# Row maxima of the attention: from two transfers per half batch to two ScalarE copies into four operand rows

## What is computed

```python
qkv = x @ w_qkv + b_qkv                       # q, k, v: 8 texts, 16 heads, 256 rows, 16 numbers
att = jnp.einsum('bhqd,bhkd->bhqk', q, k) * scale
att = jnp.where(causal, att, -jnp.inf)
att = jax.nn.softmax(att, axis=-1)            # over the keys
y = jnp.einsum('bhqk,bhkd->bhqd', att, v)
x = _layernorm(x + y @ w_proj + b_proj)
```

## Time and profile before

| what | us |
|---|---|
| three runs | 664.5, 667.37, 670.26 |
| median | 667.37 |
| span of the profiled execution | 664.9 |
| TensorE busy | 621.7 (93%) |
| VectorE busy | 493.7 (74%) |
| ScalarE busy | 327.0 (49%) |
| GpSimd busy | 225.2 (34%) |

### The profile page before, as it was taken

The page is one execution under the profiler, slowest core; times in us unless marked ns, Lnnn a source line. Parts: engine busy times, 40 slices in busy tenths (PEclk is TensorE's granted clock), DMA queues, the critical chain, the costliest instruction groups (busy, mean ns, idle before and its releaser), DMA issues.

```text
span 664.9 us, 13964 instructions
## 1 busy us (share of the span) xinstructions
PE 621.7 (93%) x5064; PEld 565.3 (85%) x5064; DVE 493.7 (74%) x1039; ACT 327.0 (49%) x734; POOL 225.2 (34%) x274
## 2 busy tenths in 40 slices
PE   5988998998999999999999999999999998899996
PEld 4766787776767989999899998999989988799996
DVE  4755474674764788879888799887999888767653
ACT  5444553553575355655556555565566644231320
POOL 9402332432453251422223232232312213352543
PEclk9799898997999999999999999999999999999999
DMA  8634646357400040010000000000000000042240
GB/s 283 203 103 146 173 135 190 93 173 217 121 18 1 1 160 0 2 33 2 0 0 0 32 0 0 0 0 0 0 1 1 1 1 1 16 147 82 80 157 34
DMA packets 31374, 43.34 MB, mean 65 GB/s; under 512 B 3072, under 2 KB 18912, under 8 KB 31328
## 3 DMA queue, kind: packets, MB, share of 16 engines
q1 hardware_dynamic: 31328, 42.73, 21.1%
HBM read 29.39 MB, written 13.21 MB: 64 GB/s over the span
## 4 chain that ended last, share of the span: by engine, by line
PE 56%; DVE 13%; issue 13%; DMA 5%; SPq 5%; POOL 4%; ACT 3%; DVEq 0%; POOLq 0%; ACTq 0%
PE bank L448 26%; PE bank L2171 11%; PE bank L1991 4%; POOL hid_hl L801 3%; DMA k_rows<-k_hl 3%; PE bank L1891 2%; DMA q_op<-negT 2%; PE bank L1977 1%; PE bank L456 1%; PE bank L1849 1%; PE bank L2008 1%; SPq L519 1%; PE bank L1856 1%; PE bank L1872 1%; PE bank L2000 1%
## 5 line engine op out<-in xcount | busy, mean ns | idle before, releaser
L448 PE MATMUL bank<-slots_hl,whhT_hl 128*128 128x256 f32 x864 | 113.1, 284 | 0.0
L448 PEld LDWEIGHTS bank<-slots_hl,whhT_hl 128*128 128x128 f32 x864 | 105.5, 188 | 2.4 <-ACT gate_z L1104 1.0
L1293 DVE TENSOR_REDUCE neg_max<-bank 128x2 f32<-128x512 f32 (+1 forms) x96 | 65.7, 690 | 55.2 <-PE bank L1858 41.3
L2171 PE MATMUL bank<-attn_hl,vg_hl 128*128 128x256 f32 x864 | 105.7, 280 | 0.1
L2171 PEld LDWEIGHTS bank<-attn_hl,vg_hl 128*128 128x128 f32 x864 | 100.9, 188 | 4.3 <-ACT attn_hl L815 3.9
L870 ACT ACTIVATE pT<-bank 128x512 f32<-128x512 f32 x96 | 56.9, 598 | 57.7 <-PE bank L1872 41.7
L682 POOL TENSOR_SCALAR_AFFINE_SELECT pT<-pT 128x512 f32<-128x512 f32 x64 | 40.6, 638 | 117.5 <-ACT pT L870 117.4
L696 POOL TENSOR_TENSOR sq<-sq 128x256 f32<-128x256 f32 x24 | 18.1, 754 | 170.6 <-ACT sq L1089 130.3
L801 POOL TENSOR_TENSOR hid_hl<-hid,hid_hl 128x512 fp32r<-128x512 f32 x32 | 40.9, 1303 | 25.8 <-ACT hid_hl L815 25.7
L448 PE MATMUL bank<-x2T_hl,keys_hl 128*128 128x256 f32 x384 | 48.6, 284 | 0.0
L448 PE MATMUL bank<-values_hl,hid_hl 128*128 128x256 f32 x384 | 47.8, 281 | 0.3 <-DVE x L1567 0.3
(11 more groups left out here) (212 smaller groups left out, 1298.2 us busy)
## 6 DMA issues: line engine op xcount, KB each, us to landing
gate_rows<-gate_mem SPq DMA_DIRECT2D x48, 128.0 KB, 3.1
q_rows<-q_hl SPq DMA_DIRECT2D x21, 256.0 KB
k_rows<-k_hl SPq DMA_DIRECT2D x21, 256.0 KB
q_op<-q_rows SPq DMA_DIRECT2D x28, 192.0 KB, 3.2
k_op<-k_rows SPq DMA_DIRECT2D x14, 384.0 KB, 4.4
x_in<-in_x_dram SPq DMA_DIRECT2D x8, 256.0 KB, 6.6
c_in<-in_ctx_dram SPq DMA_DIRECT2D x8, 256.0 KB, 4.8
out_dram<-y_out SPq DMA_DIRECT2D x8, 256.0 KB, 2.8
```

Source lines behind the costliest of these rows:

```text
L448: mm = pe.matmul(dst, left(a), right(b), start=first and n == 0, stop=last and n == 2, skip_group_check=True)
L1293: dve.tensor_reduce(dst, src, AX.X, ALU.max, negate=True).then_inc(max_ok, 1)
L2171: mm = pe.matmul(halves(b)[:, m, :], vg_hl[:, j, v_part, 3 * t + r, q:q + P], attn_hl[:, j, at_part, t, :], start=n == 2 and a + m + t == ...
```

## The change

The four maxima of a half text's pairs get four operand rows of their own, 96 to 99. A row of maxima stands in all four pairs of the queries' operand; the keys' operand has a one in row 96 + r for pair r and a zero in the other three, so that each pair picks its own. `negT`, the two transfers and the semaphores `neg_in` are gone. TensorE turns the maxima of the even and of the odd heads separately, into 4 partitions each. ScalarE copies each of the two straight into `q_op`, 4 partitions times 4 pairs times 256, at thirds 1 and 2; the second copy counts `neg_ok`. The turned matmul waits for `neg_ok`. GpSimd writes the pattern of ones at the start. In SP's queue the operand loads come first in each place, the second key write moves from place 3 to place 4, and the second x load from place 4 to place 5.

```diff
@@ -156,7 +156,6 @@
         k_op = sb("k_op", [P, 2, H // 2, T], F32R, where=s1)
         v_aug = sb("v_aug", [P, 3, NT, H, 2 * DH], where=s1)
         neg_max = sb("neg_max", [P, 2, NT, 8], where=s1)
-        negT = sb("negT", [8, 2, T], F32R, where=s1)
         stats1 = sb("stats1", [P, NT, 6], where=s1)
         mv1 = sb("mv1", [P, 2, NT, 2], where=s1)
         std1 = sb("std1", [P, 2, 2, NT], where=s1)
@@ -272,7 +271,6 @@
         ops_in = [[sem(f"ops_in{b}{h}") for h in range(2)] for b in range(2)]
         n_mm, max_ok = sem("n_mm"), sem("max_ok")
         neg_mm, neg_ok = sem("neg_mm"), sem("neg_ok")
-        neg_in = [sem(f"neg_in{h}") for h in range(2)]
         t_mm, exp_ok, sel_ok, pv_mm = sem("t_mm"), sem("exp_ok"), sem("sel_ok"), sem("pv_mm")
         a_ok, yT_mm, inv_ok, yn_ok = sem("a_ok"), sem("yT_mm"), sem("inv_ok"), sem("yn_ok")
         y_mm, y_hi, y_lo = sem("y_mm"), sem("y_hi"), sem("y_lo")
@@ -509,15 +507,6 @@
                 sp.dma_start(f32(k_op[0:K_ROWS, n % 2, pairs, :]).rearrange("p q t -> p (q t)"),
                              k_rows[n, :, :, :].rearrange("(s e) r w -> (e r) s w", e=2)[:, 2 * half:2 * half + 2, :]
                              ).then_inc(ops_in[n % 2][half], 16)
-
-            def maxima(hh):
-
-                n, half = hh // 2, hh % 2
-                sp.wait_ge(neg_ok, hh + 1)
-                after(sp, rows_ok, 2 if hh == 0 else 0)
-                for e in range(2):
-                    sp.dma_start(f32(q_op[K_ROWS:K_ROWS + 1, n % 2, e, 4 * half:4 * half + 4, :]),
-                                 f32(negT[4 * e:4 * e + 4, hh % 2, :])).then_inc(neg_in[hh % 2], 16)
 
             sp.dma_start(cols_sb[:, :], cols).then_inc(w_in[0], 16)
             sp.dma_start(st_qkv[:, 0, :, :], rows(w_qkv[0, :, :], NC)).then_inc(w_in[1], 16)
@@ -546,33 +535,23 @@
                 if quad == QUADS - 10:
                     for j in range(2):
                         sp.dma_start(c_in[:, j, :, :], ctx[j, :, :].rearrange("(t p) d -> p t d", p=P)).then_inc(c_arr[j], 16)
-                if place == 0:
-                    if 1 <= 2 * period + 1 < B:
-                        operands(2 * period + 1, 1)
-                    if 1 <= period + 1 < PAIRS:
-                        write_q(period + 1, 0)
-                    if 2 <= 2 * period < B:
-                        load_x(2 * period)
-                elif place == 1 and 1 <= period + 1 < PAIRS:
-                    write_k(period + 1, 0)
-                elif place == 2 and 2 <= 2 * period + 2 < B:
-                    operands(2 * period + 2, 0)
-                    write_q(period + 1, 1)
-                elif place == 3 and 1 <= period + 1 < PAIRS:
-                    write_k(period + 1, 1)
-                elif place == 4:
-                    if 2 <= 2 * period + 2 < B:
-                        operands(2 * period + 2, 1)
-                    if 2 <= 2 * period + 1 < B:
-                        load_x(2 * period + 1)
-                elif place == 6:
-                    if 1 <= 2 * period + 3 < B:
-                        after(sp, consts, 14 if period == -1 else 0)
-                        operands(2 * period + 3, 0)
-                    if 2 <= period + 3 < PAIRS:
-                        load_xT(period + 3)
-                if quad % 2 == 0 and 0 <= quad // 2 + 1 < 2 * B:
-                    maxima(quad // 2 + 1)
+                if place == 0 and 1 <= 2 * period + 1 < B:
+                    operands(2 * period + 1, 1)
+                elif place in (2, 4) and 2 <= 2 * period + 2 < B:
+                    operands(2 * period + 2, place // 2 - 1)
+                elif place == 6 and 1 <= 2 * period + 3 < B:
+                    after(sp, consts, 14 if period == -1 else 0)
+                    operands(2 * period + 3, 0)
+                if place in (0, 2) and 1 <= period + 1 < PAIRS:
+                    write_q(period + 1, place // 2)
+                elif place in (1, 4) and 1 <= period + 1 < PAIRS:
+                    write_k(period + 1, place // 4)
+                if place == 0 and 2 <= 2 * period < B:
+                    load_x(2 * period)
+                elif place == 5 and 2 <= 2 * period + 1 < B:
+                    load_x(2 * period + 1)
+                elif place == 6 and 2 <= period + 3 < PAIRS:
+                    load_xT(period + 3)
 
             sp.wait_ge(x1T_ok, B)
             def load_context(i):
@@ -651,14 +630,17 @@
                 pool.memset(f32(q_op[:, 1, e, :, :]), 0.0).then_inc(consts, 1)
             pool.wait_ge(consts, 14)
             for batch in range(2):
-                pool.memset(f32(k_op[K_ROWS:, batch, :, :]), 1.0).then_inc(consts, 1)
+                pool.memset(f32(k_op[K_ROWS:, batch, :, :]), 0.0).then_inc(consts, 1)
             pool.wait_ge(consts, 16)
             for batch in range(3):
                 pool.memset(v_aug[:, batch, :, :, :], 1.0).then_inc(consts, 1)
             pool.wait_ge(consts, 19)
             for e in range(2):
                 pool.memset(f32(q_op[K_ROWS:, 0, e, :, :]), 0.0).then_inc(rows_ok, 1)
-            pool.wait_ge(rows_ok, 2)
+            ones = k_op[K_ROWS:, :, :, :].rearrange("p b (h c) t -> p (b h) c t", h=2)
+            pool.affine_select(out=ones, in_=f32(ones), compare_op=ALU.not_equal, fill=1.0, base=0,
+                               pattern=[[0, 4], [-1, 4], [0, T]], channel_multiplier=1).then_inc(rows_ok, 1)
+            pool.wait_ge(rows_ok, 3)
 
             def rstd(i, var, ev, std, k, slot):
 
@@ -858,10 +840,16 @@
                     act.wait_ge(set_mm, 3 * s + e + 1)
                     copy(q_op[0:K_ROWS, 0, e, 2 * s:2 * s + 2, :], halves(set_bank(s, e))[0:K_ROWS, :, :]).then_inc(set_q, 1)
 
-            def maxima_out(hh):
+            def maxima_out(hh, e):
+
+                n, half = hh // 2, hh % 2
                 act.wait_ge(neg_mm, hh + 1)
-                after(act, neg_in[hh % 2], 32 * (hh // 2))
-                copy(negT[:, hh % 2, :], bank[BESIDE_BANK["neg", hh, 0]][0:8, 0:T]).then_inc(neg_ok, 1)
+                if e == 0:
+                    after(act, rows_ok, 3 if n == 0 else 0)
+                r = copy(q_op[K_ROWS:K_ROWS + 4, n % 2, e, 4 * half:4 * half + 4, :],
+                         halves(BESIDE_BANK["neg", hh, 0])[0:4, e, :].unsqueeze(1).to_broadcast([4, 4, T]))
+                if e == 1:
+                    r.then_inc(neg_ok, 1)
 
             def exps(quad, third):
                 act.wait_ge(t_mm, 3 * quad + third + 1)
@@ -1035,8 +1023,8 @@
                     act.wait_ge(prep_pool, 1)
                 for third in range(3):
                     key = place, third
-                    if place % 2 == 0 and third == 1 and 0 <= quad // 2 + 1 < 2 * B:
-                        maxima_out(quad // 2 + 1)
+                    if place % 2 == 0 and third > 0 and 0 <= quad // 2 + 1 < 2 * B:
+                        maxima_out(quad // 2 + 1, third - 1)
                     if key == (0, 1) and 2 <= 2 * period + 2 < B:
                         keys_hi(2 * period + 2, BESIDE_BANK["k", 2 * period + 2, 0])
                     elif key == (0, 2) and 2 <= 2 * period + 3 < B:
@@ -1865,8 +1853,7 @@
                 b = 2 + fill % 2
                 if third == 0 and quad % 2 == 0:
                     hh = quad // 2
-                    pe.wait_ge(neg_in[hh % 2], 32 * (hh // 2 + 1))
-                    after(pe, rows_ok, 2 if hh == 0 else 0)
+                    pe.wait_ge(neg_ok, hh + 1)
                 after(pe, exp_ok, fill - 1)
                 if third < 2:
                     mm = pe.matmul(halves(b), k_op[:, n % 2, pair_of(quad, third), 0:P],
@@ -1902,8 +1889,9 @@
                 if name == "neg":
                     b = bank_beside(name, n)
                     pe.wait_ge(max_ok, 6 * n + 6)
-                    for qt in range(NT):
-                        mm = pe.transpose(bank[b][0:8, qt * P:(qt + 1) * P], neg_max[:, n % 2, qt, :], ident[:, :])
+                    for e in range(2):
+                        for qt in range(NT):
+                            mm = pe.transpose(halves(b)[0:4, e, qt * P:(qt + 1) * P], neg_max[:, n % 2, qt, 4 * e:4 * e + 4], ident[:, :])
                     mm.then_inc(neg_mm, 1)
                 elif name in ("q", "k"):
                     b = bank_beside(name, n)
```

## The result

The changed kernel takes 687.92 us, the median of four runs (686.8 to 688.53); the kernel before took 667.17 in four runs beside them. The ratio is 1.0314, 95% interval 1.0285 to 1.0342: slower by 3%, which is 21 us. (A ratio compares the undisturbed runs alone, so it can differ a little from the quotient of two medians.) The forecast was slower by 1%, 676 us, with a range up to 683. The direction and the named mechanism came; the size did not, and the time lies outside the range.

A forecast was written before the change was run, and what follows sets the result against it. TensorE, busy 93% of the span, bounds the kernel. From 664.9 us: minus 12.07, plus 12.3, 2.2, 2.0, 0.9 and 4.9 for the clock gives 675.1, raised to 676; range 664 to 683.

The forecast's parts named there:

- What goes: Quads 4, 12 and 20: three TensorE waits for the maxima's transfers and the half clock go, 12.07 us gained.
- POOL idles 4.09 us before 28.03 and some before the product that precedes it, so nothing follows: Start: GpSimd's 5.1 us selection fits its idle time, costing nothing; up to 3 us if it took twice as long.
- The bank waits: Seven places in quads 0 to 18: TensorE waits for the second copy to free its bank, 1.76 us each, 12.3 together.
- The clock behind them: After the seven waits: idle of 1.49 us kept the clock, 1.78 did not; half taken at 1.4 us, 4.9.
- Transposes: TensorE, each half batch: four instead of two; two more cost 0.14 us, sixteen times 2.2; 275 ns each would make 8.8.
- Quad 14: TensorE's existing 0.93 us wait for VectorE's normalized heads grows by another 0.9 us, behind the second copy.
- smaller delays: Second copy holds ScalarE ahead of the third exponential: quads 2, 5, 13, 25 and 29 lose 2.0 us in sum.
- The SP queue: SP's issues: 32 go and loads and writes move; taken at nothing, bounds 0 and 2 us.
- the clock neither held: Rival, seven bank waits: they come but none costs clock, 670.2 us; chance 0.24.
- nor fell each time: Rival, seven bank waits: the clock falls after each, 680.0 us, or 687.8 at the longer price; chance 0.18.
- the copy was not short: Rival, ScalarE's copies: they cost only 0.36 us, each bank wait 1.10, total 662.7 us; chance 0.13.
- nothing took the old wait's place: Rival, quads 4, 12 and 20: turned matmuls still find something late, the 12 us do not return, 687 us; chance 0.05.

The follow-up runs named there:

- experiment 6: Kernel before, with SP issuing the two transfers of the maxima ahead of the query write at place 2: 671.28 us, ratio 1.0075.
- experiment 1: Kernel before, plus only GpSimd's selection over the 32 rows of ones at the start: 669.16 us, ratio 1.0054.
- experiment 2: Changed kernel, with the pattern of ones copied by ScalarE from the identity instead of selected by GpSimd: 683.2 us, ratio 1.0266.
- experiment 3: Changed kernel, with both copies of the maxima at third 1, ahead of that third's exponential: 666.53 us, ratio 1.0001.
- experiment 5: experiment 2 with the second copy, still at third 2, cut to one of its four pairs (4x256 instead of 4x1024): 669.39 us, ratio 1.0049.
- experiment 4: Kernel before, plus 24 spare ScalarE copies of 4x1024 at thirds 1 and 2 into a place nobody reads: 669.8 us, ratio 1.0046.
- experiment 7: Kernel before, with the change's order in SP's queue, the transfers of the maxima still last in each quad: 668.09 us, ratio 1.0013.
- Experiment 9: Changed kernel with both copies at third 1 and ones copied by ScalarE, but SP's old order: 666.15 us, ratio 0.9986.
- experiment 8: Changed kernel with both copies of the maxima at third 1 and the ones copied by ScalarE: 663.67 us, ratio 0.9963.

## Why the prediction was wrong

**What goes: right.** Forecast 12.07 us, measured 12.2 with the transposes counted apart. That the transfers were late because of their place in the queue is borne out: moved ahead in it, they cost TensorE 0.4 us in all (experiment 6). But there the gain is lost again at the next thing that TensorE needs, the operands.

**The failed step: "POOL idles 4.09 us before 28.03 and some before the product that precedes it, so nothing follows".** The idle time was looked for on GpSimd's own queue, and there it is; the selection is even cheaper than forecast, 3.72 for 5.1 us. What follows is on VectorE, held off its own SBUF work, so that its maxima come 2.7 us late, and then on TensorE, which waits 4.34 us for them and runs at half clock behind that wait: quad 0 starts 5.1 us late in the profile of the change and 3.5 in experiment 1, and 5.2 earlier again in experiment 2. The stated worst case was 3 us. The trace of before could have told: its 128x1536 product on VectorE takes 2.54 us beside GpSimd's product at 22.67, and 1.75 in experiment 1, where GpSimd is idle by then.

```profile
22.67 1.27 POOL L732 TENSOR_TENSOR wproj_hl<-st_proj,wproj_hl 128x512 fp32r<-128x512 f32 x1 [2.88 <-ACT eselT_hl L815]
```

```profile
23.01 2.54 DVE L1231 TENSOR_TENSOR whhT_hl<-st_hhT,whhT_hl 128x1536 fp32r<-128x1536 f32 x1
```

**The bank waits: place and number right, size a little low.** 1.76 was forecast, 1.90 measured. The copy took 1.013 us for 1.02; but no overlap with the exponential came, 0.62 from start to start instead of 0.49. Seven times: +1.0.

**The clock behind them: right in kind.** Forecast 4.9, 5.6 left over in the ledger; experiments 3 and 5 show that it hangs on the waits. Three waits of the seven lowered it, not a regular half, and its price varied. That the length of a wait settles it, as the bracket of 1.49 and 1.78 us had it, is not so: waits of 1.79, 1.89 and 2.56 us in experiment 4 and of 2.31 in experiment 7 left the clock at 1.00, and so did one of 2.61 in the kernel before itself, shown below.

**Transposes: mis-sized.** 0.23 instead of 0.14 for two more, 3.5 instead of 2.2. The prediction's own rows had it, 0.36 for four less 0.13 for two. The trace gives each some 0.27 us, the price that was weighed and set aside, but the queue advances by 0.36 for four; at full price 32 would have cost 8.8.

**Quad 14: right; smaller delays: right in sum, not in place.** Quad 14 lost 1.0 for 0.9, and experiment 4, with the load alone, lost 0.9 there. The 2.1 us of quads 21 to 31 stand against 1.1 forecast for quads 25 and 29; quads 2, 5 and 13 lost some 0.4 of their 0.9. Nor is it all the second copy's place: in experiment 3, with both copies at third 1, quads 21 to 31 still take 43.5 us, 41.0 before and 44.0 with the change.

**The SP queue: right for this kernel,** no wait for an operand came. Experiment 9, where the old order let one such wait through, suggests that the new order was not idle either.

**Not forecast: the end.** 3.0 us were lost behind the attention. Half of it is the clock, behind a wait that stands in both kernels; the changed kernel, then the one before:

```profile
585.78 0.86 PE L446 MATMUL bank<-x2T_hl,eselT_hl 128*16 128x256 f32 x6 [2.61 <-DVE x2T_hl L1219]
```

```profile
567.28 0.86 PE L448 MATMUL bank<-x2T_hl,eselT_hl 128*16 128x256 f32 x6 [2.61 <-DVE x2T_hl L1231]
```

and TensorE by stretch behind it, in the same order:

```profile
588.00:589.00 1.00, 1.00 (x7) 0.50 0.00 0
```

```profile
569.00:570.00 1.00, 1.00 (x11) 1.00 0.00 0
```

The lag behind the kernel before grows there from 18.5 to 20.0 us. Nine of the eleven traces have this drop, four of them of variants of the kernel before; the kernel before and experiment 8 do not have it. So it cannot be laid to the change: the trace that the prediction started from happened to lack it, which is bad luck. The other 1.5 us are open.

Of the miss in the span, 686.3 against 675.1, the start is 5.1, the end 3.0, transposes 1.3, waits 1.0, clock 0.7. The rivals: the clock neither held nor fell each time, the copy was not short, and nothing took the old wait's place.

## What to carry to other kernels

An engine's idle time covers new work on that engine's queue alone; ask also which other engine reads and writes the same memory in that time, and what stands behind it. A copy that releases a shared bank belongs ahead of everything in its queue that the next user need not wait for: here one place in ScalarE's order was worth 21 us, 24 such copies without the bank 3.6. And before a wait is taken away, name what TensorE needs next and when that lands: in experiment 6 it came 3.8 us sooner to operands that landed no sooner.

## What the runs showed of the hardware

- VectorE instructions within SBUF on a handful of numbers took 0.15 to 0.17 us alone and up to 2.78 beside GpSimd's selection, ending with it; a cast out of PSUM beside it kept its 0.69. Where VectorE's product had begun first, GpSimd's was held: 2.71 us for 1.27.
- Between quads 0 and 31, TensorE's waits of up to 1.50 us left its clock at 1.00, and those of 3.00 us and more had it at 0.50, in all eleven traces. In between both came: three of the changed kernel's seven waits of 1.72 or 1.73 were followed by 0.50, its 1.97 was, the 1.89, 2.31 and 2.56 named above were not. Shortening the seven from 1.72 to 1.08 or 1.09 us gave back 14.0 us, not 4.6.
- A copy of 4x1024 and an exponential follow each other without overlap (0.62 us from start to start for a duration of 0.60), and two such copies overlap by 0.10 (1.92 for two of 1.01). Why the first pair does not is open.
